# Feed-forward of an attention chunk in two halves of tokens on one PSUM bank, with three banks for the scores

## The reference

```
x = x + softmax(scale * (q.k * tau + delta)) v Wo      # 16 heads of 16, q from LN(x), k and v from ctx
x = x + top-1 expert of 8 (router on LN(x)) * its router probability
x = x + tanh([windowed attention over ctx, LN(x)] Wc)  # a window of ctx around p_t, masked, times a gaussian
x = x + slot router (gelu, top 8 of 64 slots, softmax) -> slots: GRU step, attention, LN -> back to tokens
```

## Time and profile before

| | us |
|---|---|
| time, median of 3 runs | 1086.86 (1086.31 to 1095.68) |
| time of the profiled execution | 1086.41 |
| its span, first to last instruction | 1084.4 |
| PE busy / DVE busy / ACT busy | 978.2 (90%) / 745.5 (69%) / 571.3 (53%) |
| granted TensorE clock, mean | 0.968 of 2.4 GHz |

### The profile page before, as it was taken

How to read it: one execution, slowest core, us unless ns; L and a number is a source line. 1 busy time by engine, 2 the same in 40 slices (tenths; PEclk the granted TensorE clock), 3 DMA queues, 4 the chain that set the end, 5 groups by cost and what they waited for, 6 DMA issues and landing times.

```text
span 1084.4 us, 13614 instructions
## 1 busy us (share of the span) xinstructions
PE 978.2 (90%) x4794; PEld 390.6 (36%) x4794; DVE 745.5 (69%) x1704; ACT 571.3 (53%) x1063; POOL 63.8 (6%) x91
## 2 busy tenths in 40 slices
PE   6799999999889999989889989989989999889986
PEld 3453323323333334423323333423333333334643
DVE  4688888887677777776677777776767764235634
ACT  2456766666454456665445546665445547740330
POOL 3441000000000000000000000000000000100000
PEclk9899999999899989999899989999899989999999
DMA  7936500001000000001000000001000000140022
GB/s 187 200 73 111 121 1 15 16 1 35 1 16 1 16 1 14 3 1 55 1 16 1 15 1 13 3 1 54 1 15 1 0 2 1 40 125 2 1 97 78
DMA packets 33931, 36.19 MB, mean 33 GB/s; under 512 B 6670, under 2 KB 30523, under 8 KB 33603
## 3 DMA queue, kind: packets, MB, share of 16 engines
q1 hardware_dynamic: 32542, 34.17, 12.5%
q10 hardware_dynamic: 1242, 0.90, 0.6%
q0 software_dynamic: 80, 0.26, 0.1%
HBM read 21.55 MB, written 7.35 MB: 27 GB/s over the span
## 4 chain that ended last, share of the span: by engine, by line
issue 51%; PE 30%; DVE 9%; DMA 2%; ACT 2%; POOL 2%; DVEq 2%; SPq 1%; POOLq 0%; ACTq 0%
PE ps_m L1064 7%; PE ps_o L1148 7%; PE ps_e L1350 5%; DVE mx L1651 4%; PE ps_e L1022 2%; DMA xres<-in_x 1%; PE ps_m L1350 1%; SPq L545 1%; PE ps_m L1168 1%; PE ps_m L1298 1%; POOL rstd L684 1%; POOL xres L735 1%; PE ps_m L1301 1%; DVE xn L1643 1%; DMA x<-xres 1%
## 5 line engine op out<-in xcount | busy, mean ns | idle before, releaser
L1651 DVE TENSOR_REDUCE mx<-ps_m 128x1 f32<-128x401 f32 x1024 | 538.3, 568 | 198.0 <-PE ps_m L1064 190.6
L848 ACT ACTIVATE probs<-ps_e 128x512 f32<-128x512 f32 (+1 forms) x763 | 437.1, 598 | 342.2 <-PE ps_e L1350 340.5
L1064 PE MATMUL ps_m<-k_stack,q_stack 99*128 99x401 bf16 x1024 | 319.4, 343 | 36.6 <-DVE mx L1651 34.9
L1350 PE MATMUL ps_e<-q_stack,k_stack 101*128 101x512 bf16 (+1 forms) x763 | 299.5, 394 | 10.9 <-ACT probs L848 8.7
L1148 PE MATMUL ps_o<-probs,v_heads 128*32 128x512 f32 (+1 forms) x1664 | 228.9, 623 | 0.0
L1350 PEld LDWEIGHTS ps_e<-q_stack,k_stack 101*128 101x128 bf16 (+1 forms) x763 | 75.9, 100 | 261.8 <-ACT probs L848 167.7
L1064 PEld LDWEIGHTS ps_m<-k_stack,q_stack 99*128 99x128 bf16 x1024 | 102.0, 100 | 183.8 <-DVE mx L1651 131.0
L1252 PE MATMUL ps_m<-expert_w,xnT 128*128 128x512 f32 x192 | 99.4, 598 | 15.2 <-DVE xb L1788 15.2
L1148 PEld LDWEIGHTS ps_o<-probs,v_heads 128*32 128x32 f32 (+1 forms) x1664 | 33.1, 109 | 60.7 <-issue 49.4
L848 ACT ACTIVATE probs<-ps_m 128x512 f32<-128x512 f32 (+1 forms) x69 | 41.6, 603 | 15.2 <-PE ps_m L1350 15.1
L1788 DVE SCALAR_TENSOR_TENSOR xb<-ps_m,hot,xb 128x256 f32<-128x256 f32 x84 | 40.6, 484 | 7.9
(11 more groups left out here) (333 smaller groups left out, 720.0 us busy)
## 6 DMA issues: line engine op xcount, KB each, us to landing
q_stack<-q_parts SPq DMA_DIRECT2D x78, 64.0 KB, 2.6
expert_w<-in_expert_wT SPq DMA_DIRECT2D x2, 1024.0 KB, 12.9
xres<-in_x SPq DMA_DIRECT2D x4, 512.0 KB, 3.8
x<-xres SPq DMA_DIRECT2D x4, 512.0 KB, 3.2
probs<-x SPq DMA_DIRECT2D x1, 2048.0 KB, 8.5
k_stack<-alphaT SPq DMA_DIRECT2D x10, 200.1 KB, 7.6
probs<-in_ctxT SPq DMA_DIRECT2D x3, 512.0 KB, 7.5
q_parts<-probs SPq DMA_DIRECT2D x4, 384.0 KB, 3.0
```

The costliest lines, as they stand in the source:

```text
L848: act.activation(probs[0:n, k % 2, h, :], score_bank(c, k, h)[0:n, :], ACT.Exp).then_inc(s["exp_done"], 1)
L1064: pe.matmul(ps_m[:, (UNITS * n1 + u) % RING, 0:SPLIT], qst[0:MAX_ROW, g, h, P * t:P * t + P], kst[0:MAX_ROW, HG * g + h, QUARTER_START[q]: ...
L1350: pe.matmul(score_bank(c, k, h)[0:n, :], kst[0:ROWS, HG * g + h, P * st:P * st + n], qst[0:ROWS, g, h, :], start=True, stop=True).then_inc ...
L1651: dve.tensor_reduce(mx[:, q, col:col + 1], ps_m[:, (UNITS * n1 + u) % RING, 0:SPLIT], AX.X, ALU.max)\
```

## The change

Chunks 0 to 2 now use the two halves too. Per half and chunk there is one generator, and a third (`choice`) for the slot router, which stays whole; all three run in every quarter. All jobs go through one bank (`bank` is `ps_m[:, RING]`), and `bank_free` waits for the job right before. The other job bank becomes a third score bank in all chunks. Semaphores are split by half. Experts are filled in 256-column matmuls at AT and AT+1 and taken at AT+2 and AT+3, with hold 4; there are 8 per half, so 16 as before. `normal_half` stands one quarter ahead of its `t` job.

```diff
-JOBS = [("ota", None, 10, 3), ("otb", "ota", 2, 3), ("y0", "otb", 3, 3), ...
+HALF_STEPS = [("ot", None, 10, 3), ("y", "ot", 3, 3), ("t1", "y", 8, 3), ("router", "t1", 3, 2), ("e0", "router", 7, 4),
+              ("e1", "e0", 4, 4), ("gateT", "e1", 4, 2)]
+HALF_STEPS += [(f"e{i}", f"e{i - 1}", 4, 4) for i in range(2, NE // 2)]
+HALF_STEPS += [("gb", f"e{NE // 2 - 1}", 4, 4), ("t2", "gb", 8, 3), ("score", "t2", 3, 3), ("aT", "score", 9, 3), ("z", "aT", 3, 5), ("t3", "z", 11, 3)]
+LAST_STEPS = [("h", "t3", 3, 4), ("logits", "h", 4, 2), ("slots", "logits", 13, 5), ("alphaT", "slots", 5, 3)]
...
         def bank(job, c):
-            return ps_m[:, RING + JOB[job, c][0], :]
+            return ps_m[:, RING, :]
         def bank_free(eng, job, c):
-            b, n = JOB[job, c]
-            need(eng, bank_taken[b], n)
+            need(eng, s["bank_taken"], JOB[job, c])
...
         def score_bank(c, k, h):
-            return ps_e[h % 2] if c else (*ps_e, ps_x)[(HG * k + h + 1) % 3]
+            return (*ps_e, ps_x)[(HG * (SLOTS * c + k) + h + 1) % 3]
...
+            def expert_half(i, c, h):
+                half_free(pe, f"e{i}", c, h)
+                tok, j = HC * h + P * (i // 4), i % 4
+                for e in range(2):
+                    for k in range(KT):
+                        if e and not k:
+                            yield AT[f"e{i}", h] + 1
+                        mm = pe.matmul(half_bank(f"e{i}", c, h)[:, D * e:D * e + D], xnT[:, k, tok:tok + P],
+                                       expert_w[:, k, CT * j + D * e:CT * j + D * e + D], start=(k == 0), stop=(k == KT - 1))
+                fills_half(mm, f"e{i}", c, h)
...
-                        need(pe, s["exp_done"], HG * SLOTS * c + HG * k + h - (1 if c else 2))
+                        need(pe, s["exp_done"], HG * SLOTS * c + HG * k + h - 2)
...
+                yield AT["t1", h] - 1
+                normal_half(xa, 0, c, h)
```

More of the change, by code:

```diff
@@ L180, in job_numbers, with go_on, at_once @@
                 order.append(("o", NG * c + O_AT.index(q) - 1))
-        if c == 0:
-            first = len(order)
-        else:
+        if c:
             order += [(name, c - 1) for name in AT if AT[name] >= HG * SLOTS]
     order.append(("o", NG * NC - 1))
-    numbers = {job: (0, i) for i, job in enumerate(order[:first])}
-    numbers.update({job: (1 - i % 2, i // 2 + (first if i % 2 else 0)) for i, job in enumerate(order[first:])})
-    return numbers
+    return {job: i for i, job in enumerate(order)}
 def begin(steps):
     return [steps, next(steps)]
-def go_on(work, quarter):
-    while work and work[1] <= quarter:
-        work[1] = next(work[0], NEVER)
+def go_on(works, quarter):
+    for work in works:
+        while work[1] <= quarter:
+            work[1] = next(work[0], NEVER)
+def at_once(steps):
+    for _ in steps:
+        pass
 JOB = job_numbers()
@@ L438, in half_free @@
[L438 to L454, removed]
@@ L914, in chunk @@
             def chunk(c):
-                work = begin(behind(c - 1)) if c else None
+                work = [begin(steps) for steps in (behind(c - 1, 0), behind(c - 1, 1), choice(c - 1))] if c else []
                 for k in range(SLOTS):
@@ new lines, in norm_turned, with rows_half @@
+            def norm_turned(i, c, h):
+                pe.wait_ge(xn_half[h], 3 * c + i + 1)
+                yield from turned_half(f"t{i + 1}", c, h, xn)
+            def rows_half(name, c, h, after, rows, weights):
+                wait_half_taken(pe, after, c, h)
+                half_free(pe, name, c, h)
+                for t in range(HT):
+                    if t:
+                        yield AT[name, h] + t
+                    for k in range(KT):
+                        mm = pe.matmul(half_bank(name, c, h)[:, D * t:D * t + D], rows[:, k, HC * h + P * t:HC * h + P * t + P],
+                                       weights[:, k, :], start=(k == 0), stop=(k == KT - 1))
+                fills_half(mm, name, c, h)
@@ L1219, in behind @@
+            def behind(c, h):
+                yield AT["ot", h]
+                if c == 0 and h == 0:
                     pe.wait_ge(s["ld_fill"], N_FILL)
@@ new lines, in behind @@
+                router_half(c, h)
+                for i in range(NE // 2):
+                    yield AT[f"e{i}", h]
+                    yield from expert_half(i, c, h)
+                    if i == 1:
+                        yield AT["gateT", h]
+                        gates_half(c, h)
+                yield AT["gb", h]
+                yield from bias_half(c, h)
+                yield AT["t2", h]
+                yield from norm_turned(1, c, h)
+                yield AT["score", h]
+                yield from rows_half("score", c, h, "t2", xnT, win_k)
@@ L1740, in behind @@
[L1740 to L1755 removed]
+                last.then_inc(var_half[h], 1)
@@ L1822, in behind @@
[L1822 to L1830 removed]
+                last.then_inc(a_half[h], 1)
```

982 lines of the change are left out of this document (415 added, 567 removed).

## The result

The changed kernel takes **1173.38 us** (median of 4 runs, 1172.36 to 1174.21), the kernel before 1087.07 (1086.31 to 1095.68): a ratio of 1.077, with 95% interval 1.072 to 1.083. It is 86 us slower. The direction was forecast, the size was not: 1112 with a range to 1142.

What follows compares the result with a forecast made beforehand. TensorE's in-order queue in chunks 1 to 3 was taken as the bound. Hand-overs less savings gave 28 - 17 = 11 us each in chunks 1 and 2, 24 - 21 = 3 in chunk 3: 25 more, 1112 us, range 1070 to 1142.

Steps and rivals of the forecast that it cites:

- rival 3: Slower by clock: stretches at 1.2 GHz double, 9 us a chunk more, 1139 us; chance 0.21 together with the upper bound.
- Hand-overs: TensorE waits for the single job bank: net cost 28 us each in chunks 1 and 2, 24 in chunk 3.
- Phase 1: Expert jobs starting in phase 1 wait for DVE's take of the job before: 0.8 us each, seven a chunk.
- phase 2: Jobs starting in phase 2 wait for DVE's take: 1.7 us each, 2.1 by the sum, three a chunk.
- phase 3: Jobs starting in phase 3 (into router', aT) wait for DVE: 2.1 us each, two a chunk.
- phase 0: Jobs starting in phase 0, with the value products between: 0.69 us at quarter 64, three a chunk.
- the jobs behind `o`: Three hand-overs a chunk behind `o`, each 0.43 us and a short operation: 1.05 us each.
- Scores: The third score bank lets scores run two exponentials behind: saves 6 us each in chunks 1 and 2, 13 in chunk 3.
- Maxima: Halves split DVE's bunches, so max matmuls wait less: saves 11 us each in chunks 1 and 2, 8 in chunk 3.
- Clock: Granted clock in these chunks taken as unchanged, since hand-overs of 1.5 us had brought no fall.
- Tail: Expert matmuls' doubled weight loads are hidden, costing 0 to 0.5 us in the tail.
- upper bound: Hand-overs net 33 us, savings 14: 19 + 19 + 10, 1135 us; chance 0.21 together with rival 3.

Runs made afterwards that it cites:

- e2: The changed kernel with halves kept, but the earlier kernel's two job banks and two score banks in chunks 1 to 3: 1084.35 us.
- e1: The changed kernel with scores of chunks 1 to 3 on two banks again, jobs still on the single bank: 1185.10 us.
- e13: e1 plus two unread 512-column f32 matmuls ahead of the waits of each turned and expert job: 1226.54 us.
- e14: e1 plus two unread 128-column f32 matmuls ahead of the waits of each turned and expert job: 1184.30 us.
- e12: e11 with both halves of an expert's bank taken by VectorE in the same quarter, the second one a quarter earlier: 1087.70 us.
- e11: e7 with the logits matmul two quarters later: 1074.20 us.
- e7: e2 with each half's normalised rows made two quarters ahead of their transposes, not one: 1074.07 us.

## Why the prediction was wrong in size

**The mechanism was right.** The chain "a job on the single bank waits for DVE's or ACT's take of the quarter before, with all scores and maxima behind it" is what e2 against e1 and the timelines show. Most of the signs named ahead are there: in chunk 1 twelve expert matmuls wait for DVE, 12.9 us together (7.6 + 5.3 in the waits above; 12 to 17 were forecast); the first expert matmul of the tiles of quarters 65 to 77 idles 0.85 to 0.94 us (0.6 to 0.8); tiles without max work at the end of chunk 3 take 2.46 us where no job stands in them (2.2 to 2.4); PEclk is 0.94 in chunk 1, right at the mark for rival 3. One sign is missing: the waits of the max loads, 17.3 us in chunk 1, did not fall to a few us.

**The steps that failed are sizes in the sum.** It was 80 of hand-overs less 55 of savings, with nothing for the clock. Measured are 101 of hand-overs, 14 of clock and 2 in the tail, less 33 of savings. Its terms, one by one:

- *Hand-overs, net 28, 28 and 24.* Measured 34, 34 and 33 (50, 50 and 50 less 16, 16 and 17). The list added up nearly rightly: the single waits over 0.5 us before jobs of chunk 1 come to 42 us in the changed kernel and 11 before, where I had 43 and 11. Phase 1 cost 0.85 to 1.05 (0.8 forecast), phase 2 2.28 and 2.04 (1.7, where the upper value of 2.1 was the better one), phase 3 2.04 and 2.06 (2.1), phase 0 0.61 and 0.68 (0.7), the jobs behind `o` 0.93 to 1.03 (1.05). But in part this was luck, since single prices were far off in both directions. The logits, 0.65 for an ACT copy, wait 2.32, and the slots, 1.43, were not on the list; e0 (0.7) waits 0.04, and e2 and e2' (1.6 each) 0.99. Two subtractions were wrong. I took off a tenth, 4 us, because DVE would sometimes be ahead, though the list already came out at what was measured. DVE itself waits for maxima that stand behind the same job, 83.9 us in chunk 1. And in chunk 3 I took off 4 us more for its quarter without maxima; its job waits are 50 us like the others. The remaining 2 to 3 us a chunk are gaps of some 0.1 us inside jobs, 8 us after and 5 before, which no term had.
- *Scores, 6, 6 and 13 saved.* Measured 5, 5 and 6.5 of waits, and 12 us of time from e1. The chunk 3 term was twice too large. I took 13 of its 15.6 us for the exponentials that the earlier trace rows show in tiles without max work, but only a quarter of the tiles is free of max work. By the starts of the matmuls 8 us of score waits stood in these tiles before, and 4 are still there with three banks.
- *Maxima, 11, 11 and 8 saved.* Measured 5.5, 5 and 5.5. **Of the savings this term failed furthest**, 30 us against 16: the halves split DVE's bunches of operations as I said, but I took 11 of 14 us on the strength of one row of 2.28 us. e2 shows that this saving comes from the halves alone (22 us of max waits there, 39 before), and that they give more than half of it back at the scores and jobs (5 us each).
- *Clock, 0.* Measured 14 us by the table, 12 by the runs' clocks. I took the earlier trace rows for the forecast, where single waits of 1.5 us brought no fall, and set aside. With 50 us of job waits in a chunk instead of 16 the stretches at 1.2 GHz add up to 78 us in the three chunks, where they had 48 before; which wait brings a fall isn't shown. Rival 3 had the mechanism, with twice the size, 27. The Trainium skill's TensorE: Matmul & The Clock Gate, "A second HAM failure mode: psum-queue depth-cycling", says that short idle times of TensorE between groups of matmuls make the clock fall and rise again and again. e13 and e14 agree in kind: with the gaps filled the clock column falls from 41 to 19 and 32.
- *Tail, 0 to 0.5.* Measured 2 us. The smaller expert matmuls did not cause them: TensorE's streaming at full clock is the same there (85.7 and 85.9 us), its waits are 0.5 us longer, and stretches at 1.2 GHz add 6.0 us instead of 4.2. These 2 us are clock too.

The logits' wait is ACT's table load of 1.28 us ahead of the gelu of 0.69, and not a copy; the first line is the end of the exponentials, the last is the logits' first matmul:

```profile
492.89 1.08 ACT L866 ACTIVATE probs<-ps_e 128x512 f32<-128x512 f32 x2 [1.82 <-PE ps_e L1350]
493.99 1.28 ACT L924 ACT_TABLE_LOAD   x1
495.28 0.69 ACT L924 ACTIVATE hT<-ps_m,hbias 128x512 f32<-128x512 f32 x1
...
496.12 1.25 PE L1323 MATMUL ps_m<-w,hT 128*128 128x64 f32 x6 [2.14 <-ACT hT L924]
```

Hand-overs were 21 us too small, the clock 14, the savings 22 us too large, the tail 2 more: 59 of the 61 us between forecast and result. No single term would have brought it into the range. All the errors point the same way: the savings were taken high in their waits, the discounts went to the cost, and the clock was left at 0. The upper bound that I gave, 1135, had the hand-overs at 43 in full but the clock at 0 as well, and rival 3 had the clock but the forecast's hand-overs and savings; no case held both. By the table it is 34 a chunk of hand-overs, where my upper bound was 33, 11 of savings, where my lowest were 14, and 5 of clock, between the forecast's 0 and rival 3's 9: together 28 a chunk (34 - 11 + 5).

**What the change's two parts are worth.** Halves on two banks: 2 us less than the kernel before in the runs beside it, which the interval does not tell from nothing. The second job bank taken away: +101, its share of the clock included. The third score bank: -12. The last two belong together, since PSUM has no further bank: a score bank can be bought only with the job bank. Full-width jobs on a single bank were not run: the same planner with one bank would put their last job at quarter 283 of a chunk that has 208.

**What stays open.** Which stretches fall to 1.2 GHz, and why e12 loses 8 us to it that e11 doesn't, and e7 9 us less than e2.

## What to carry to other kernels

A ring of two banks between TensorE and the engines that empty it is worth far more than a third bank where two are there: 101 us against 12 here, because TensorE's queue is in order and whatever waits in it holds everything behind, the inputs of the very engine that is waited for included. When a job waits for two things, find the later one before moving the earlier (it took nothing off the transposes' waits at `t3` on one bank, and 12 us off all of them on two), and price a hand-over by all that stands in the emptying engine's queue in that quarter, not by the length of its last operation. And in a sum of costs and savings, take both from the same side of their bounds, and have one case that adds the clock to the upper bound: here it was 14 us.

## What the runs showed of the hardware that I had not expected

- A mean granted clock of 0.01 less goes with 8.5 us over an otherwise identical kernel of 1085 us (59 executions; a straight line through them accounts for 97% of the variance of the span). The differences of a few us from run to run are nearly all clock, and so a comparison of two profiled executions should state their clocks.
- Filling TensorE's waits with matmuls that nobody reads can cost nearly nothing: 33 us of them in e14 left the time where it was (1184.3 against 1185.1 us). It did not pay either.
- An f32 matmul of 512 columns takes 0.85 us of TensorE's time, in two instructions, four times that of bf16 scores of the same width (0.21).
